# Rows finished by the last expert that picks them, stored partly ahead, and a ninth place for one weight chunk

## What is computed

```
x = x + 0.5 * ffn(layernorm(x))
x = x + attn(layernorm(x))
x = x + 0.5 * ffn(layernorm(x))
```

```
idx   = top_k(softmax(x @ gate_w.T + gate_b, over rows), 8)
h     = gelu(merged @ w1[e] + b1[e])
o     = h @ w2[e] + b2[e]
out[row picked] += o * weight
```

## Time and profile before

| | us |
|---|---|
| median of 3 runs (2336.25 to 2341.73) | 2341.41 |
| the profiled execution | 2340.34 |
| its span, first to last instruction | 2338.6 |

### The profile page before, as it was taken

One profiled execution on the slowest core, in us unless ns is written; L12 is line 12 of the kernel. 1 busy time (PEld: TensorE's weight loads), 2 busy tenths in 40 slices (PEclk: granted clock), 3 DMA queues, 4 the chain that ended last, 5 costly groups with the idle time before them and its releaser, 6 DMA issues.

```text
span 2338.6 us, 44296 instructions
## 1 busy us (share of the span) xinstructions
PE 1995.7 (85%) x18716; PEld 1183.0 (51%) x18716; DVE 737.4 (32%) x1245; ACT 817.8 (35%) x1539; POOL 644.6 (28%) x779
## 2 busy tenths in 40 slices
PE   5799999999999999899999999999666556666655
PEld 4556666666666666677667667666411111111111
DVE  6731111111111111567767767767310000000002
ACT  6831211211111111577777777777300000000000
POOL 7610000000000000477777777777220000000002
PEclk9899999999999999999999999999887887777787
DMA  9999999999999999375544544544599999999994
GB/s 366 343 383 404 418 425 421 423 423 420 427 419 423 425 419 364 92 239 183 165 148 147 165 148 150 162 139 135 223 422 425 425 424 425 423 425 425 424 424 194
DMA packets 130709, 762.22 MB, mean 326 GB/s; under 512 B 21156, under 2 KB 21156, under 8 KB 77264
## 3 DMA queue, kind: packets, MB, share of 16 engines
q1 hardware_dynamic: 118736, 701.35, 76.1%
q10 hardware_dynamic: 9216, 50.34, 5.2%
q0 software_dynamic: 2560, 7.70, 0.8%
HBM read 648.09 MB, written 105.91 MB: 322 GB/s over the span
## 4 chain that ended last, share of the span: by engine, by line
PE 57%; DMA 24%; POOL 8%; ACT 6%; issue 3%; SPq 1%; DVE 1%; POOLq 0%; ACTq 0%; DVEq 0%
PE ps L297 53%; DMA big<-in_L_ffn_w 24%; PE ps L301 3%; POOL big L1440 2%; POOL s L1443 2%; ACT big L587 1%; POOL big L1414 1%; POOL s L1425 1%; ACT big L1267 1%; SPq L18 1%; ACT big L570 1%; POOL big L1445 1%; POOL big L1437 1%; PE ps L764 1%; ACT big L575 1%
## 5 line engine op out<-in xcount | busy, mean ns | idle before, releaser
L297 PE MATMUL ps<-big 128*32 128x512 f32 (+4 forms) x13776 | 988.5, 420 | 243.5 <-DMA big<-in_L_ffn_w 205.2
L297 PEld LDWEIGHTS ps<-big 128*32 128x32 f32 (+2 forms) x13776 | 387.7, 128 | 740.0 <-issue 370.4
L305 DVE TENSOR_TENSOR big<-ps,big 128x128 f32<-128x128 f32 (+3 forms) x373 | 342.5, 933 | 742.2 <-PE ps L764 565.7
L297 PE MATMUL ps<-wth,xth 128*128 128x512 f32 x768 | 312.2, 407 | 0.0
L297 PE MATMUL ps<-wtl,xth 128*128 128x512 f32 x768 | 299.9, 390 | 0.0
L297 PE MATMUL ps<-wth,xtl 128*128 128x512 f32 x768 | 299.7, 390 | 0.0
L805 ACT COPY big<-ps 128x512 f32<-128x512 f32 x64 | 37.5, 586 | 652.8 <-PE ps L297 652.8
L1432 POOL TENSOR_SCALAR big<-big 128x1 f32<-128x1 f32 x64 | 12.2, 190 | 855.6 <-ACT ps L1245 853.2
L951 ACT ACTIVATE big<-ps,big 128x512 f32<-128x512 f32 x128 | 88.2, 689 | 375.5 <-PE ps L297 359.1
L960 DVE TENSOR_SCALAR big<-ps,big 128x512 f32<-128x512 f32 x64 | 48.1, 751 | 535.9 <-PE ps L297 535.9
L297 PE MATMUL ps<-wo,s 128*128 128x512 f32 x768 | 210.4, 409 | 3.4 <-ACT big L1315 1.9
(11 more groups left out here) (124 smaller groups left out, 1774.0 us busy)
## 6 DMA issues: line engine op xcount, KB each, us to landing
big<-in_L_ffn_w SPq DMA_DIRECT2D x256, 2048.0 KB, 19.0
p_scratch<-big ACTq DMA_DIRECT2D x64, 768.0 KB, 10.7
big<-p_scratch SPq DMA_DIRECT2D x64, 768.0 KB, 5.8
big<-in_L_attn_x SPq DMA_DIRECT2D x68, 256.0 KB, 3.0
xt_scratch<-big SPq DMA_DIRECT2D x16, 1024.0 KB, 8.5
big<-xt_scratch SPq DMA_DIRECT2D x16, 1024.0 KB, 16.1
x_weight_scratch<-big SPq DMA_DIRECT2D x64, 256.0 KB, 3.3
out_x<-big SPq DMA_DIRECT2D x64, 256.0 KB, 3.6
```

Of the source, the lines that this page charges most:

```text
L297: return nc.tensor.matmul(o, l, r, start=start, stop=stop, skip_group_check=True)
L305: return nc.vector.tensor_tensor(o, p, q, op)
```

## The change

1. **Ownership.** EARLIER becomes LATER, the triangle the other way round: a row belongs to the *last* expert that picks it. IDX is otherwise as before, and all 16 gathers stay; they now also wait until chunk 3 has been used.
2. **The last four experts' rows are set apart.** A second list, IDXA, is IDX with all picks of experts 28 to 31 (LAST = 28) moved beyond the array. These picks' indices (2 x 128) go to a DRAM array and back as IDXB, one per partition (last_rows_sp, at the end of SP's expert 4: eight stores of 4 x 8 numbers, a wait until they have landed, two loads). POOL gathers these rows again, into XB.
3. **Finishing ahead.** At expert 28, behind scatter group 6, DVE writes O with what experts 0 to 27 have given (s_sel 15), and final_pe and final_dve treat 5, 5 and 6 of the 16 columns at the ends of experts 28, 29 and 30, now with two banks of PSUM in place of four. POOL stores columns 0 to 7 (EARLY = 8) as they come; from column 8 on it waits until the last weight chunk has landed.
4. **At the end** only two columns are left: last_pe, last_dve and two stores by IDXB.
5. **A ninth place.** Chunk 3 goes to the place where attention keeps its outer products' copies (OS), which is free once the last tile's products are read (s_c = 64). It is loaded in SP's iteration 62 of the attention. This place is used once. Chunks 4 to 8 take the points in SP's program that chunks 3 to 7 had, and experts_sp loads g+9.
6. The weights' transposes move from experts 16 to 31 to experts 12 to 27.

```diff
+        ring = [at(SLOT * i, SLOT) for i in range(8)] + [at(os_at, SLOT)]
+        LAST = 4 * (E // 4 - 1)
+        EARLY = 8
         def slot_of(g):
+            if g < 4 * E:
+                return g % 4
+            return g - 4 * E + 4 if g < 4 * E + 3 else 8 if g == 4 * E + 3 else (7, 2, 0, 1, 3, 4, 5, 6)[(g - 4) % 8]
...
-                    ahead = 8 if p else 4
+                    ahead = 9 if p else 4
                     if (g + ahead) // (4 * E) == p:
                         load_chunk(sp, g + ahead)
+                if p == 1 and e == 4:
+                    last_rows_sp(sp)
...
+                if p == 1 and LAST <= e < E - 1:
+                    for i in ((0, 1, 2, 3, 4), (5, 6, 7, 8, 9), (10, 11, 12, 13, 14, 15))[e - LAST]:
+                        final_pe(pe, i)
...
+                if p == 1 and e == 0:
+                    late_dve(dve)
+                if p == 1 and 12 <= e < LAST:
+                    weight_dve(dve, e - 12)
+                if p == 1 and e == LAST:
+                    dve.wait_ge(s_sel, 15)
+                    dve.wait_ge(d_b2, 128)
+                    for h in range(2):
+                        tt(O[:, h, :], ps[:, 6 + h, :], B2, ALU.add).then_inc(s_o, 1)
+                    weight_last_dve(dve)
...
+                if n == NT - 2:
+                    sp.wait_ge(s_c, NT)
+                    load_chunk(sp, 4 * E + 3)
...
+        def last_rows_sp(sp):
+            sp.wait_ge(s_own, 20)
+            for h in range(2):
+                for q in range(4):
+                    r = 128 * h + 32 * q
+                    sp.dma_start(lastd[r:r + 32, :].rearrange("(e j) a -> e (j a)", j=8),
+                                 IDX[32 * q + LAST:32 * q + E, 8 * h:8 * h + 8]).then_inc(d_last[0], 16)
+            sp.wait_ge(d_last[0], 16 + 16 * 8)
+            for h in range(2):
+                sp.dma_start(IDXB[:, h:h + 1], lastd[128 * h:128 * h + 128, :]).then_inc(d_last[1], 16)
...
         def final_pool(pool):
             for i in range(16):
                 pool.wait_ge(s_fout, i + 1)
+                if i == EARLY:
+                    pool.wait_ge(d_ring[slot_of(8 * E - 1)], 16 * turn[8 * E - 1])
...
+            for h in range(2):
+                pool.wait_ge(s_fout, 17 + h)
+                nc.gpsimd.indirect_dma_start(
+                    out=outr, out_offset=bass.IndirectOffsetOnAxis(ap=IDXB[:, h:h + 1], axis=0),
+                    in_=XB[h][:, 0:D], in_offset=None,
+                    bounds_check=B * S - 1, oob_is_err=False).then_inc(d_fs, 16)
+            pool.wait_ge(d_fs, 16 * 20)
```

More of the change, by code:

```diff
@@ L36, in macaron_block @@
     xmd = nc.dram_tensor("x2_weight_scratch", (B * S, XW), F).ap()
+    lastd = nc.dram_tensor("last_scratch", (256, 1), mybir.dt.uint32).ap()
     xs = x.rearrange("b (c p) d -> (b c) p d", p=128)
@@ L100, in at @@
             return t.take(n)
-        ring = [at(SLOT * i, SLOT) for i in range(8)]
+        ring = [at(SLOT * i, SLOT) for i in range(8)] + [at(os_at, SLOT)]
         def halves(name, p, n):
@@ L160, in macaron_block @@
         PICK, RANK = M[0][:, 0, :], M[0][:, 1, :]
+        XB = [M[0][:, h, 0:XW] for h in range(2)]
+        WB2 = [M[0][:, h, 576:608] for h in range(2)]
+        LAST = 4 * (E // 4 - 1)
+        EARLY = 8
         WT = [BK[:, 32 * i:32 * i + 32] for i in range(16)]
@@ L793, in scatter_pe @@
             pe.wait_ge(s_pt, 8 * p + G + 1)
+            if p == 1 and G == 7:
+                pe.wait_ge(s_o, 4)
             for half in range(2):
@@ L1493, in rank_dve @@
                                            op1=ALU.add).then_inc(s_own, 1)
+            nc.vector.scalar_tensor_tensor(out=IDXA[:, 8 * h:8 * h + 8], in0=T8, scalar=ROW0A[h], in1=NONE,
+                                           op0=ALU.add, op1=ALU.add).then_inc(s_own, 1)
         def gather_pool(pool):
@@ L1509, in weight_dve, with final_pe @@
             nc.vector.transpose(WT[i], XS[i][:, D:XW]).then_inc(s_twt, 1)
-        def final_pe(pe):
+        def final_pe(pe, i):
+            h = i // 8
             pe.wait_ge(s_twt, 16)
[L1513 to L1516, removed]
+            pe.wait_ge(s_o, 4)
+            pe.wait_ge(s_fout, i - 1)
+            for q in range(4):
+                R_ = slice(32 * q, 32 * q + 32)
+                t = mm(ps[R_, 2 + i % 2, :], WT[i][R_, :], O[R_, h, :], True, True)
+            t.then_inc(s_fin, 1)
@@ new lines, in final_dve, with weight_last_dve, last_pe @@
+        def final_dve(dve, i):
+            dve.wait_ge(s_fin, i + 1)
+            nc.vector.scalar_tensor_tensor(out=XS[i][:, 0:D], in0=ps[:, 2 + i % 2, :], scalar=0.5,
+                                           in1=XS[i][:, 0:D], op0=ALU.mult, op1=ALU.add).then_inc(s_fout, 1)
+        def weight_last_dve(dve):
+            dve.wait_ge(d_fs, 16 * 2)
+            for h in range(2):
+                nc.vector.transpose(WB2[h], XB[h][:, D:XW]).then_inc(s_twt, 1)
+        def last_pe(pe):
+            pe.wait_ge(s_twt, 18)
+            pe.wait_ge(s_fout, 16)
+            for h in range(2):
+                pe.wait_ge(s_o, 5 + h)
@@ L1517, in final_pe, with last_dve @@
                 for q in range(4):
                     R_ = slice(32 * q, 32 * q + 32)
-                    t = mm(ps[R_, i % 4, :], WT[i][R_, :], O[R_, h, :], True, True)
+                    t = mm(ps[R_, 2 + h, :], WB2[h][R_, :], O[R_, h, :], True, True)
                 t.then_inc(s_fin, 1)
[L1522 to L1526, removed]
+        def last_dve(dve):
+            for h in range(2):
+                dve.wait_ge(s_fin, 17 + h)
+                nc.vector.scalar_tensor_tensor(out=XB[h][:, 0:D], in0=ps[:, 2 + h, :], scalar=0.5,
+                                               in1=XB[h][:, 0:D], op0=ALU.mult, op1=ALU.add).then_inc(s_fout, 1)
```

71 lines of the change are left out of this document (47 added, 24 removed).

## The result

The changed kernel takes 2326.54 us (median, 2325.79 to 2326.89), the kernel before 2341.41 us: a ratio of 0.9942, 95% interval [0.9928, 0.9957]. The forecast was 2327.0, from 2319 to 2335. The medians in this document leave out three executions, one of them of the kernel before, that took 2582 to 3778 us.

What follows compares the result with a forecast made beforehand. The weight stream bounds the second pass, then store issues the tail. -4.93 + 4.0 + 1.35 + 4.1 - 18.35 = -13.85 us from the profiled 2340.34 gives 2326.5; adjusted towards the median of runs, 2327.0, range 2319 to 2335.

Steps and rivals of the forecast that it cites:

- ninth place: Second pass's weight stream: chunk 3 loaded during attention puts the saturated stream one chunk ahead, -4.93 us.
- wait in SP's queue: Expert 4: SP waits some 36 us for eight tiny stores behind queued chunks, the stream runs dry, +4.0 us.
- second gather: Weight stream: fetching the last four experts' rows again, about 250 rows at their packets' time, +1.35 us.
- eight early stores: Weight stream: POOL's first eight column stores now fall into it and cost their packets' time, +4.1 us.
- last chunk, from S: Last weight chunk lands 4.5 us later; S, used in measuring, is the start of DVE's last merge addition.
- tail: After the last chunk: nine steps of POOL's stores and one stall, 17.8 us in place of 36.15, -18.35.
- What bounds it: Second pass bound by the weight stream near 425 GB/s, then the tail by the pace of store issues.
- the tail's pace: Rival: early stores hold up the stream at the tail's pace, 13.4 us instead of 4.1; 2336 to 2340, chance 0.15.
- Edits at nothing: DVE steps, the gathers' wait, moved transposes and columns at experts 28 to 30 lie under the stream: 0 us.
- the slower rival: PE stays at 1.2 GHz through experts 28 to 31 and becomes the bound: 2343 or 2358 us, chance 0.05.

Runs made afterwards that it cites:

- alone, undone: Kernel before with only the ninth place added: 2335.28 us against 2339.93; changed kernel with the ninth place taken out: 2330.95 us.
- the repeat: Changed kernel with SP's wait and index loads moved to expert 16, run again on another chip: 2325.19 us, 2322.56 the first time.
- moved, alone: Changed kernel, SP's wait and index loads moved to expert 16: 2322.56 us; kernel before with only the eight small stores and their wait: 2344.06 us.
- gathers by IDXA: Changed kernel with SP's wait at expert 16 and the sixteen gathers reading IDXA: 2323.43 us, against 2325.19 without the IDXA edit.
- EARLY = 0: Changed kernel with all sixteen of POOL's column stores waiting for the last chunk: 2335.10 us.
- EARLY = 8, 11, 12 and 16: Early store counts: 8 and 16 in the changed kernel, 2326.54 and 2325.51 us; 11 and 12 with wait at expert 16 and IDXA gathers, 2321.90 and 2320.08.

## Why the prediction was right, point by point

| term | predicted us | measured us | by |
|---|---|---|---|
| ninth place | -4.93 | -4.65 and -4.4 in time, -5.1 and -4.4 in the stream | alone, undone |
| wait in SP's queue | +4.0 | 4.0 (1.3 in the repeat, with its later S) and 4.1 in time, 3.6 (4.1 in the repeat) and 3.0 in the stream, holes of 4.6 and 4.5 | moved, alone |
| second gather | +1.35 | open (1.8 in time, of which 1.2 are S; nothing in the stream) | gathers by IDXA |
| eight early stores | +4.1 | +4.2 in the stream | EARLY = 0 |
| last chunk, from S | +4.5 | +4.2 | the changed kernel |
| tail | -18.35 | -17.95 | the changed kernel |

**What bounds it** was right: the stream up to the last chunk, then POOL's issues. That one chunk ahead gives one chunk's time holds with and without the rest of the change.

**The wait** had its mechanism and its size right, and its course partly wrong. It lasted 31.6 us from the first small store's issue, and 24.2 from the end of the last one's issue, which is what the table of waits counts, where 36 had been said, and it stood at 1805 us and not near 1825: chunk 28 is issued earlier than I had counted. Also the small stores' own issue took 7.36 us for eight, not the 0.43 each that I had from an emptier queue. None of this matters for the hole, which starts when the queue is dry. As the ninth place gave about 4.6 and the wait took about 4, these two parts of the change nearly cancel; the gain comes from the tail.

**The early stores** cost what their packets' time said, 4.2 for 4.1. The gathers were the right row to price them by, and the tail's pace (13.4) the wrong one.

**The tail** was right in its parts: nine steps and one stall took 13.6 us (2306.69 to 2320.31) where 13.7 had been said, and the end came 3.8 us behind the last issue, as said. It was 0.45 us longer than the 17.8 of the prediction, since the ninth store came 0.85 us after the landing and not 0.3.

**The second gather** is the one term that no run bears out: with fewer rows to fetch the last chunk landed no earlier. Without it the terms measured in the stream add up to between 2.1 and 3.9 us, against the 4.2 of the changed kernel; what is left, 0.3 to 2.1 us, is the second gather and all edits priced at nothing together.

**The number** came closer (2326.54 for 2327.0) than its working deserves: S alone lies between 1681.84 and 1686.52 us in the traces, and one kernel gave 2322.56 and 2325.19. That is luck; the sizes of the terms are not.

**Edits at nothing.** PE at the end of expert 30 (start, us, what), in the changed kernel:

```profile
2286.24 13.95 PE L310 MATMUL ps<-big 128*32 128x512 f32 x96 [2.18 <-DMA big<-in_L_ffn_w]
2300.90 0.75 PE L779 MATMUL ps<-big 128*128 128x128 f32 x4 [0.71 <-ACT big L825]
2302.37 1.92 PE L310 MATMUL ps<-big 128*32 128x512 f32 x16 [0.72 <-ACT big L833]
2305.89 1.92 PE L310 MATMUL ps<-big 128*32 128x512 f32 x16 [1.59 <-DMA big<-in_L_ffn_w]
```

It works through expert 30's last chunk, six columns and expert 31's first two chunks in one piece, at a mean granted clock of 0.78 from 2286 to 2300 us. For the last chunk it waits 1.59 us: its lateness is gone, at the high clock (1.92 us for a chunk's matmuls), as the case against the slower rival had it.

## What to carry to other kernels

Where a stream of loads is the bound, price every edit by what it does to the stream: one buffer more, filled while the DMA engines are idle ahead of it, is worth one load's time, once; a wait on a small transfer in the queue that issues the loads costs a dry queue, here some 4 us for eight stores of 4 x 8 numbers, and it goes away if the queue issues the transfer early and asks for it much later. Where a tail is a row of issues on one engine, work that can be finished per part belongs under the stream, and even paid for in the stream at its packets' time (4.2 us for eight stores here) it was cheaper than its issues in the tail (12.4 us, 2.1 of them a stall).

## What the runs showed that I had not expected

POOL's stall counts issues. In all thirteen traces it fits the 7th, 15th, 23rd and 30th indirect transfer of the pass, gathers and stores counted together: with 16 gathers behind the 7th and 14th store, with 18 transfers ahead of the stores behind the 12th (EARLY = 8, 11, 12 and 16), and with EARLY = 0 behind the 5th and 12th; where stores go early, POOL mostly waits for the next columns behind the 5th anyhow. Fewer rows by IDXA leave the places as they are, so it goes by transfers and not by bytes. The seventh and eighth gather of the kernel before:

```profile
1719.35 1.00 POOL L1502 DMA_INDIRECT big<-x_weight_scratch,idx  x1 [0.30 <-issue]
1736.93 1.01 POOL L1502 DMA_INDIRECT big<-x_weight_scratch,idx  x1 [16.58 <-issue]
```

In a quiet stretch POOL is idle there for 2.3 us in place of 0.3, in the gathers beside the stream for up to 16.6. Why it stalls, no run here shows. The number of transfers ahead decides whether a tail holds a stall.

A small store's issue behind a full queue is slow: eight took 7.36 us, and 13.59 in the kernel before with the wait alone, 9.60 of it for the first, where a store's issue near the end of attention takes 0.43.

With the ninth place alone the tail of the profiled execution, which is 1.7 us above that kernel's median, was 1.8 us longer than before (2335.3 - 2297.34 = 37.96 us). PE's four scatter matmuls there, and before:

```profile
2300.86 3.78 PE L300 MATMUL ps<-big 128*128 128x512 f32 x4 [0.69 <-ACT big L828]
```

```profile
2306.34 1.98 PE L297 MATMUL ps<-big 128*128 128x512 f32 x4 [0.69 <-ACT big L825]
```

From 2300 to 2303 us the granted clock was 0.50, the low level of 1.2 GHz; before, it was 0.95 from 2306 to 2310. The last chunk's own matmuls were 0.4 us shorter (2.79 and 3.20), so PE made 1.4 of the 1.8 us. A tail that goes through PE depends on the clock that PE happens to have in it.
